# Bounds of the scatters in registers set once, and the final wait moved from SyncE to GpSimd, in a vision-transformer layer with routed experts

## The reference

```python
h = tok(x); h = concat([cls_tok, h], axis=1)
h = h + attn(layernorm(h))
# experts, on z = layernorm(h), 592 tokens of 256
gates = softmax((z @ w_red) @ normalized(wg).T)
idx = argmax(gates); scores = gates[idx]
y = gelu(z @ w1[idx] + b1[idx]) @ w2[idx] + b2[idx]
out = h + y * scores
```

## Time and profile before

| | us |
|---|---|
| median of 3 runs | 133.79 |
| the three runs | 133.21, 134.04, 133.79 |
| the profiled execution, whole time | 133.21 |
| its span in the profile | 131.3 |
| TensorE busy in the span | 123.1 |
| GpSimd busy in the span | 41.1 |

### The profile page before, as it was taken

The page is one execution under the profiler, slowest core; times in us unless marked ns, Lnnn a source line. Parts: engine busy times, 40 slices in busy tenths (PEclk is TensorE's granted clock), DMA queues, the critical chain, the costliest instruction groups (busy, mean ns, idle before and its releaser), DMA issues.

```text
span 131.3 us, 2718 instructions
## 1 busy us (share of the span) xinstructions
PE 123.1 (94%) x1034; PEld 105.2 (80%) x1034; DVE 58.2 (44%) x179; ACT 48.2 (37%) x143; POOL 41.1 (31%) x52
## 2 busy tenths in 40 slices
PE   5999999999999999999899999999999999999960
PEld 1768897887667777777799998999998989999840
DVE  1231899363986898888957000522102121220210
ACT  0300002383866745662349360066042331506000
POOL 8800034850092193314847500050020202011022
PEclk9999999999999999999999999999999999999999
DMA  4899999159469999999996548999999994000000
GB/s 125 276 394 407 379 411 403 56 176 182 96 138 185 242 362 387 364 386 358 400 352 248 228 124 229 355 405 371 397 362 386 350 377 143 24 0 24 2 28 30
DMA packets 19934, 33.37 MB, mean 254 GB/s; under 512 B 1799, under 2 KB 13704, under 8 KB 19918
## 3 DMA queue, kind: packets, MB, share of 16 engines
q1 hardware_dynamic: 18382, 30.73, 70.8%
q0 software_dynamic: 768, 2.12, 4.3%
q10 hardware_dynamic: 768, 0.31, 0.9%
HBM read 27.75 MB, written 5.84 MB: 256 GB/s over the span
## 4 chain that ended last, share of the span: by engine, by line
PE 68%; DMA 14%; DVE 7%; issue 4%; POOL 3%; SPq 2%; ACT 1%; POOLq 0%
PE ps L793 22%; PE ps L807 19%; PE ps L524 9%; DMA w2s<-v_scratch 5%; DMA early<-embed_in 4%; DMA v_scratch<-hz 4%; PE ps L584 4%; PE ps L591 3%; POOL vbd L1118 2%; PE ps L672 2%; PE ps L685 2%; PE ps L715 2%; PE ps L654 1%; SPq L341 1%; PE ps L776 1%
## 5 line engine op out<-in xcount | busy, mean ns | idle before, releaser
L507 ACT ACTIVATE early<-ps,b1s 128x128 f32<-128x128 f32 x64 | 18.2, 370 | 31.7 <-PE ps L793 31.7
L793 PEld LDWEIGHTS ps<-early,w1s 128*128 128x128 f32 x256 | 29.4, 192 | 0.4 <-issue 0.2
L793 PE MATMUL ps<-early,w1s 128*128 128x128 f32 x256 | 29.6, 275 | 0.0
L807 PE MATMUL ps<-w2s,early 128*128 128x256 f32 x128 | 28.8, 379 | 0.0
L807 PEld LDWEIGHTS ps<-w2s,early 128*128 128x128 f32 x128 | 23.8, 190 | 2.9
L524 PE MATMUL ps<-early 128*128 128x256 f32 x60 | 15.4, 408 | 0.5 <-DMA early<-embed_in 0.5
L524 PEld LDWEIGHTS ps<-early 128*128 128x128 f32 x60 | 11.8, 204 | 3.5 <-DMA early<-embed_in 1.8
L1051 DVE COPY early<-ps 128x256 f32<-128x256 f32 x6 | 2.5, 425 | 25.9 <-PE ps L776 25.9
L1143 POOL DMA_INDIRECT out<-pos,early x4 | 3.9, 970 | 25.7 <-DVE pos L1067 25.3
L1143 POOL DMA_INDIRECT out<-pos,wide x4 | 3.9, 973 | 21.1 <-DVE pos L1067 21.1
L591 PE MATMUL ps<-xnt,wqkv 128*128 128x296 f32 x32 | 9.1, 422 | 0.0
(11 more groups left out here) (132 smaller groups left out, 168.1 us busy)
## 6 DMA issues: line engine op xcount, KB each, us to landing
w1s<-w SPq DMA_DIRECT2D x8, 1024.0 KB, 10.7
w2s<-w SPq DMA_DIRECT2D x8, 1024.0 KB, 12.2
slot_scratch<-nil SPq DMA_DIRECT2D x1, 2560.0 KB, 15.1
early<-embed_in SPq DMA_DIRECT2D x5, 448.0 KB, 7.2
early<-slot_scratch SPq DMA_DIRECT2D x4, 320.0 KB, 5.4
wide<-slot_scratch SPq DMA_DIRECT2D x4, 320.0 KB, 6.6
b2s<-b SPq DMA_DIRECT2D x4, 256.0 KB, 8.0
wqkv<-w_qkv SPq DMA_DIRECT2D x1, 768.0 KB, 10.7
```

The lines of the kernel that those rows point to most:

```text
L507: nc.scalar.activation(gt[:, t % 2, f, :], ps[:, 2 * (t % 2) + f // 4, (f % 4) * P:(f % 4 + 1) * P], ACT.Gelu, bias=b1t[:, f:f + 1]).then_ ...
L793: m = nc.tensor.matmul(ps[:, 2 * (t % 2) + f // 4, (f % 4) * P:(f % 4 + 1) * P], w1s[:, r, k, f * P:(f + 1) * P], xt[:, t % 2, k, :], star ...
L807: m = nc.tensor.matmul(ps[:, 4 + t % 2, 0:D], gt[:, t % 2, f, :], w2s[:, r, f, :], start=(f == 0), stop=(f == FT - 1))
```

## The change

In the two helpers that issue indirect DMAs on GpSimd, the bound given as a number becomes a register. The two registers are set by `to_reg` ahead of the first wait for `ids_ready`, once for all. And the two waits for the scatters leave the end of SyncE's program and stand at the end of GpSimd's, behind its last `If`.

```diff
@@ -383,8 +383,6 @@
                     sp.wait_ge(scattered[i % 2], 16 * (i // 2 + 1))
                     sp.dma_start(row_of(E + i), slot_d[bass.ds(row, P), :]).then_inc(gathered[i], 16)
-            for b in range(2):
-                sp.wait_ge(scattered[b], 16 * E // 2)
 
@@ -1136,13 +1134,15 @@
                 pool.indirect_dma_start(slot_d, bass.IndirectOffsetOnAxis(keyu[0:n, j:j + 1], 0), hz[0:n, j, :], None,
-                                        bounds_check=(E + 1) * APART - 1, oob_is_err=False).then_inc(q["spread"], 16)
+                                        bounds_check=last_place, oob_is_err=False).then_inc(q["spread"], 16)
 
             def scatter(t):
                 pool.wait_ge(q["y_ready"], t + 1)
                 pool.indirect_dma_start(out, bass.IndirectOffsetOnAxis(row_of(t).bitcast(U32)[:, 2 * D:2 * D + 1], 0), yout[:, t % 2, :], None,
-                                        bounds_check=T - 1, oob_is_err=False).then_inc(scattered[t % 2], 16)
-
+                                        bounds_check=last_token, oob_is_err=False).then_inc(scattered[t % 2], 16)
+
+            last_place = pool.to_reg((E + 1) * APART - 1)
+            last_token = pool.to_reg(T - 1)
             pool.wait_ge(q["ids_ready"], 1)
@@ -1163,6 +1163,8 @@
                     scatter(E + i)
                     pool.wait_ge(scattered[i % 2], 16 * ((E + i) // 2 + 1))
+            for b in range(2):
+                pool.wait_ge(scattered[b], 16 * E // 2)
```

## The result

The changed kernel takes 134.44 us (median of 22 runs) beside 133.70 us for the kernel before (22 runs too); the ratio is 1.0048, with a 95% interval of 1.0026 to 1.0071. By the ratio that is 0.64 us more (0.35 to 0.95), by the two medians alone 0.74; 0.8 us less was forecast. The change goes the other way than forecast. That the number still lies in the range of 132.4 to 134.6 us is no merit of the mechanism: the range had been drawn to take in rival 1, on whose side the number is.

What follows compares the result with a forecast made beforehand. TensorE's full stretch was taken as fixed, so only the tail counted: 0.15 start, 2.3 landing, 0.04 waits, 0.38 DRAIN, 0.2 to the end, 3.07 us in all, 0.8 us less; 133.0 us on the median, range 132.4 to 134.6.

Steps and rivals of the forecast that it cites:

- rival 1: At the program's end: scatter starts 0.64 us earlier, but a fixed 1.50 us DRAIN follows the landing; 134.1 us, chance 0.27.
- What bounds the kernel, and where the change can act: TensorE is full from 69 to 124.4 us; only the 3.9 us tail, ended by GpSimd's DRAIN, can change.
- Part 1, the place of the wait: Last scatter on GpSimd: without the MOVE it waits in the queue and starts 0.64 us earlier (0.03 to 0.70).
- the bound of 0.21: Last scatter on GpSimd: 0.21 us from y_ready to its start if all behind the hold remains; 0.15 was taken.
- ScalarE's row: ScalarE's count load starts at 120.0 beside four activations ahead of it, read as a sequencer running past a waiting instruction.
- Part 2, the DRAIN: End of GpSimd's program: the DRAIN starts only after the landing and takes 0.38 us, between 0.17 and 0.6.
- The two waits: End of GpSimd's program, ahead of its DRAIN: the moved waits take about 0.02 us each, 0.04 together.
- The landing: Last scatter: its landings are complete 2.3 us after its start, as before the change.
- The threshold of 1.2 us: GpSimd's DRAIN behind the wait: if longer than 1.2 us, the change loses despite the scatter's early start.

Runs made afterwards that it cites:

- e3: The kernel before with five more DRAINs on GpSimd in its idle times; run once, for its profile, 133.65 us.
- e8: The kernel before once more, with no edit, run once for its profile; 135.08 us.
- e1: The kernel before with only the bounds in registers, the final wait staying in SyncE's program; 133.67 us, ratio 0.9963 to the kernel before.
- e2: The kernel before with only the final wait moved to GpSimd, the bounds staying numbers; 134.68 us, ratio 1.0058 to the kernel before.
- e4: e1 with GpSimd's count load and overflow-spread If ahead of the last scatter, and one If around the overflow scatters; ratio 0.9994 to the kernel before.
- e5: e1 with a wait for the landing and one DRAIN on GpSimd behind scatter 5; 133.34 us, ratio 0.9962 to the kernel before.
- e7: e1 with TensorE's overflow tiles (count load and four untaken branches) left out; run once, for its profile, 133.56 us.
- e10: e5 with TensorE's overflow tiles left out; 132.59 us, ratio 0.9915 to the kernel before.

## Why the prediction was wrong

- **What bounds the kernel, and where the change can act**: right. TensorE's work on the experts takes the same 57.77 us, and GpSimd's DRAIN, not SyncE's wait, set the end before.
- **Part 1, the place of the wait**: right in kind, 0.52 us measured for 0.64 taken. The start came 0.28 us after y_ready, just beyond the bound of 0.21. The picture behind it was half wrong: the sequencer does its work on the scatter ahead of the wait, but stays with it, so the count load began 0.04 us after y_ready and not before. I had misread ScalarE's row. Of the four activations only the first carries a wait, and the count load behind them starts at 119.98, 0.03 us after the semaphore of that wait (119.95), although its own had been raised at about 72. That row already showed a held sequencer, not one that runs past a waiting instruction. This cost nothing here: the branches still ended (129.2) well ahead of the landing. The page of the Trainium skill that I cited, "Perfetto Trace Analysis", section "DMA Instruction — SWDGE (GPSIMD)", has the sequencer free while the instruction waits; here it is not free, and the measurement decides.
- **Part 2, the DRAIN**: this is the step that failed. I put it at 0.38 us behind the landing, between the 0.17 of an idle GpSimd and the 0.6 that stick out beyond the landing now. It takes 1.14 us. My argument that it holds for something outstanding was right (7.0 us in e3), and it would have been right for one scatter (0.11 to 0.14 us). It left out that the DRAIN also has work that grows with the indirect DMAs since the last DRAIN, about 0.084 us for each. For thirteen of them that is 1.10 us, of which 0.55 us (1.14 less 0.59) had been hidden under the last flight, and the change took that cover away. My bound "0.6 us, what it takes now beyond the landing" was not a bound: a length read behind a cover is only the part that sticks out.
- **The two waits**: 0.04 us taken; from the landing to the start of the DRAIN it is 0.24 us, with a branch between wait and DRAIN that I had seen on SyncE and not counted. With the DRAIN's 0.55 us this makes the 0.79 us.
- **The landing**: 2.3 us taken as fixed; 2.9 in the profiled execution, a miss almost as large as the DRAIN's there. It changes with the packets of the instruction queue, in the kernel before as well (e8).
- **Rival 1** had 0.3 us more, with the right place and a wrong reason (a fixed length of 1.50 us). The threshold of 1.2 us that I gave it was computed with the small start and the short waits. With what was measured, 0.28 + 2.27 + 0.24 + 0.24 us around the DRAIN, the change loses as soon as the DRAIN is longer than 0.87 us; it is 1.14, so by these terms, with a landing on time, 0.27 us are lost, which is also about the sum of e1 and e2. So the DRAIN and the waits turn the sign without any late landing. But 0.27 lies just below the interval of the whole change (0.35 to 0.95 us). That late landings, more frequent with the earlier scatter, make up the rest is likely and not shown.

## What to carry to other kernels

A wait moved ahead of another instruction costs what that instruction had hidden under the waiting, so the length of the instruction behind it has to be known uncovered; measure it alone before the move. On GpSimd, in all twelve profiles here, the indirect DMAs left work for the next DRAIN, and a DRAIN in an idle time of the engine, behind a landing, took it off the end of the program. A register written once, instead of between a wait and a scatter, let the sequencer's half microsecond on the scatter pass before its input was there.

## What the runs showed of the hardware

- GpSimd's DRAIN, with all its indirect DMAs landed, took 46 ns with none since the last DRAIN, 113 and 136 ns with one, 218 with two, 973 with eleven (four profiles), 1143 with thirteen (two profiles): 46 ns and 84.4 ns for each, within 17 ns. Begun beside the flight, it ended 0.12 us after the last landing with two (four profiles), 0.42 us with nine (e3) and 0.59 us with thirteen (five profiles), even when it began 3.0 us before that landing (e4).
- GpSimd's sequencer spent 0.52 us on an indirect DMA, ahead of the DMA's own wait where no other instruction carried that wait (0.28 us from y_ready to the start, against 0.80 with a MOVE between), and it was held until the wait was met: what stood behind, a load or a branch (e4), began 0.04 us after y_ready.
- Beside a packet of the instruction queue, 16 KB and 0.95 to 1.5 us long, the sixteenth landing of the last scatter came 1.05 us behind the packet's end, up to 1.0 us later than the other fifteen, even where that end lay before the scatter's own packets (e3, e5). With no such packet all sixteen came within 1.32 us (e7, e10).
